# Routing the last batch in two groups of half a batch, unchecked expert ids and earlier writes of q and k, in a fused attention and mixture-of-experts kernel

## The reference

```
x1 = layernorm(x + attention(x))
scores = sigmoid(x1 @ router_weight.T)            # 16 experts, in 4 groups of 4
# the best 2 groups by scores + bias, in them the best 4 experts: tidx
tw = scores[tidx] / sum(scores[tidx]) * 2.5
h_e = silu(x1 @ gate_w[e].T) * (x1 @ up_w[e].T)   # 128 wide, for each expert e
out = layernorm(x1 + sum over the 4 chosen of tw * (h_e @ down_w[e].T)
                   + shared(x1))                   # 2 shared experts, for every token
```

## Time and profile before

| | us |
|---|---|
| median of three runs | 1260.3 |
| lowest and highest | 1251.3 and 1264.51 |
| profiled execution, its own time | 1256.9 |
| its span in the profile | 1254.9 |
| PE busy, share of the span | 1056.3, 84% |
| DVE busy | 863.1, 69% |
| ACT busy | 626.5, 50% |
| POOL busy | 469.5, 37% |

### The profile page before, as it was taken

How to read it: one execution, slowest core, us unless ns; L and a number is a source line. 1 busy time by engine, 2 the same in 40 slices (tenths; PEclk the granted TensorE clock), 3 DMA queues, 4 the chain that set the end, 5 groups by cost and what they waited for, 6 DMA issues and landing times.

```text
span 1254.9 us, 24541 instructions
## 1 busy us (share of the span) xinstructions
PE 1056.3 (84%) x8451; PEld 590.1 (47%) x8451; DVE 863.1 (69%) x1833; ACT 626.5 (50%) x1409; POOL 469.5 (37%) x682
## 2 busy tenths in 40 slices
PE   7696999989777998988997779888898776998895
PEld 4353333344422555544554445454555445654463
DVE  6486787777884666788667676687567556587453
ACT  4323677766444555654555456554455463322332
POOL 7552111152156102223444633214625630286332
PEclk9897999999897999999999899999999898998998
DMA  5753257420123433234366634232636643443320
GB/s 177 214 173 109 69 198 267 125 68 26 49 89 116 62 92 76 58 71 97 98 155 113 169 75 89 61 76 79 150 94 137 181 104 70 136 121 107 90 76 21
DMA packets 181078, 136.07 MB, mean 108 GB/s; under 512 B 105152, under 2 KB 156096, under 8 KB 180960
## 3 DMA queue, kind: packets, MB, share of 16 engines
q1 hardware_dynamic: 170112, 106.17, 33.2%
q0 software_dynamic: 9216, 25.18, 6.4%
q10 hardware_dynamic: 1632, 3.15, 0.9%
HBM read 54.55 MB, written 60.88 MB: 92 GB/s over the span
## 4 chain that ended last, share of the span: by engine, by line
PE 50%; DVE 17%; POOL 12%; issue 11%; ACT 5%; SPq 3%; DMA 2%; DVEq 0%; POOLq 0%; ACTq 0%
PE bank L752 10%; PE bank L575 10%; PE bank L559 8%; PE bank L546 7%; DVE a_mx L1275 5%; POOL a_pool L1076 4%; PE bank L765 3%; PE bank L709 2%; POOL a_QS L1068 2%; POOL rows L1061 2%; ACT a_PT L1137 2%; POOL a_PT L1020 2%; PE bank L659 1%; SPq L838 1%; PE bank L723 1%
## 5 line engine op out<-in xcount | busy, mean ns | idle before, releaser
L1275 DVE TENSOR_REDUCE a_mx<-bank 128x1 f32<-128x512 f32 (+3 forms) x720 | 423.8, 619 | 224.2 <-PE bank L549 144.9
L1137 ACT ACTIVATE a_PT<-bank 128x512 f32<-128x512 f32 (+4 forms) x832 | 374.7, 497 | 224.9 <-PE bank L559 221.3
L559 PE MATMUL bank<-a_QS,a_KS 113*128 113x512 f16 (+4 forms) x832 | 279.8, 344 | 40.3 <-DVE a_mx L1275 32.7
L1020 POOL TENSOR_SCALAR_AFFINE_SELECT a_PT<-a_PT 128x256 f32<-128x256 f32 (+1 forms) x288 | 111.5, 394 | 471.8 <-ACT a_PT L1137 471.1
L546 PE MATMUL bank<-a_KS,a_QS 112*128 112x512 f16 (+4 forms) x832 | 264.6, 340 | 10.4 <-DMA a_KS<-k_dram 5.6
L575 PE MATMUL bank<-a_PT,a_VG 128*17 128x512 f32 (+4 forms) x1664 | 188.3, 527 | 26.6 <-POOL a_PT L1020 26.6
L752 PE MATMUL bank<-e_xt,a_W 128*128 128x128 f16 x1728 | 139.6, 231 | 40.1 <-issue 28.7
L752 PEld LDWEIGHTS bank<-e_xt,a_W 128*128 x1728 | 118.5, 102 | 67.9 <-issue 52.4
L559 PEld LDWEIGHTS bank<-a_QS,a_KS 113*128 113x128 f16 x832 | 82.8, 101 | 121.6 <-DVE a_mx L1275 65.4
L546 PEld LDWEIGHTS bank<-a_KS,a_QS 112*128 112x128 f16 x832 | 81.2, 100 | 103.0 <-ACT a_PT L1137 64.5
L1223 ACT ACTIVATE e_tq<-bank 128x256 f32<-128x256 f32 x96 | 36.8, 383 | 173.1 <-PE bank L752 172.9
(11 more groups left out here) (176 smaller groups left out, 1476.8 us busy)
## 6 DMA issues: line engine op xcount, KB each, us to landing
outs<-e_ys SPq DMA_DIRECT2D x72, 256.0 KB, 2.9
rows<-a_pool SPq DMA_DIRECT2D x48, 256.0 KB, 3.2
a_QS<-c_dram SPq DMA_DIRECT2D x32, 256.0 KB, 3.3
q_dram<-p_qk SPq DMA_DIRECT2D x32, 128.0 KB, 2.1
k_dram<-p_qk SPq DMA_DIRECT2D x32, 128.0 KB, 2.3
v_dram<-p_vs SPq DMA_DIRECT2D x8, 512.0 KB, 3.6
a_QS<-q_dram SPq DMA_DIRECT2D x64, 64.0 KB
a_KS<-k_dram SPq DMA_DIRECT2D x64, 64.0 KB
```

The lines of the kernel that those rows point to most:

```text
L559: pe.matmul(ps[:, 0:(qc + 1) * CH - q0], KS[p][0:MR + 1, kt // NT, h % 2, kt % NT * P:kt % NT * P + P], QS[p][0:MR + 1, qc, h, q0 - qc * C ...
L1020: pool.affine_select(out=a, in_=a, compare_op=ALU.is_ge, fill=0.0, base=q0 - (kt * P - WIN), pattern=[[0, 2], [1, w]], channel_multiplier= ...
L1137: act.activation(PT[(G + i) % 2][:, h, 0:w], bank("ST", G, i, h)[:, 0:w], ACT.Exp)\
L1275: dve.tensor_reduce(mx[:, piece, t // NT, heads[0]:heads[0] + n, t % NT], bank("S", G, u)[:, 0:n * w].rearrange("p (h k) -> p h k", h=n), ...
```

## The change

1. The last batch is routed, in two groups of its own, one for each chunk: 4 tiles, 16 full units of choices and 16 partly filled ones, 32 units, 16 pairs. The five groups are `GROUPS`; the dense jobs (`up`, `down`, `cT`, `dgate`, `load_c` and the rest) are gone. `slot`, `expert` and `wk` get a third buffer.
2. From h = 416 on `fill` takes turns in seven banks, and the pairs from `LATE` on load their rows into 8 tiles that lie in the softmax's buffers PT, which are free once the attention has ended.
3. `load_experts` leaves out the check of the ids against 0 and 15.
4. SP writes chunks 2, 3 and 4 ahead of `stack(0, 0)`.
5. In the first four rounds S takes banks 0 to 2, ST banks 3 to 5, and `fill` bank 7 alone.

```diff
+GROUPS = [(b, 0, BT) for b in range(B - 1)] + [(B - 1, half * NT, NT) for half in range(NH2)]
+UNITS_OF = [TOPK * n + NE for _, _, n in GROUPS]
...
             def load_experts(b, n):
                 on.wait_ge(f["unit_done"], b + 1)
                 _, regs = nc.values_load_multi_w_load_instructions(
-                    expert[b % 2][0:1, n:n + REGS], engines=[mybir.EngineType.PE], min_val=0, max_val=NE - 1)
+                    expert[b % 3][0:1, n:n + REGS], engines=[mybir.EngineType.PE], min_val=0, max_val=NE - 1,
+                    skip_runtime_bounds_check_because="the ids are counts of experts that are held to at most NE - 1")
...
-    RINGS = {"scores": [0, 1, 2, 3, 4], "other": [5, 7], "project": [5, 6, 7], "gates": [0, 1], "ups": [2, 3],
-             "sum0": [4], "sum1": [6]}
+    RINGS = {"s_first": [0, 1, 2], "st_first": [3, 4, 5], "first": [7], "scores": [0, 1, 2, 3, 4], "other": [5, 7], "project": [5, 6, 7], "gates": [0, 1], "ups": [2, 3],
+             "end": [5, 7, 0, 1, 2, 3, 4]}
...
-                ring = "other"
+                ring = "first" if h < 2 * NG * NSL else "other" if h < 2 * ATT else "end"
...
+    def rows_in(i):
+
+        if i < LATE:
+            return xt[i % NXT][:], xt_loaded[i % NXT], i // NXT * 16 + 16, i - NXT
+        j = i - LATE
+        return late_tiles[j % NXL], xt_late[j % NXL], j // NXL * 16 + 16, i - NXL if j >= NXL else -1
...
+            for c in range(2, 5):
+                project(c)
             for p in range(2):
                 sp.wait_ge(qk_written[p], 128)
                 sp.wait_ge(v_written[p], 16)
...
-            for c in range(2, NC - 1):
+            for c in range(5, NC - 1):
                 project(c)
...
+    w = 0
+    for g in range(NGR):
+        at = max(last[g] + 6, w)
+        if g == B - 2:
+            at = max(at, routed[NGR - 1] + 1)
```

More of the change, by code:

```diff
@@ L86, in share, with chunk_of, shared_place @@
     return [((n - TAIL) % NU, n >= TAIL) for n in range(lo, hi)]
[L89 to L99, removed]
+def chunk_of(g, tile):
+    b, j0, _ = GROUPS[g]
+    return b * NH2 + (j0 + tile) // NT
+def shared_place(g, n):
+    return chunk_of(g, n // NSH * 2), n // NSH * 2 % NT
 def plan():
@@ L169, in plan @@
     ready, routed = {}, {}
[L170 to L177, removed]
+    for g, (b, j0, tiles_) in enumerate(GROUPS):
+        late = b == B - 1
+        for c in sorted({chunk_of(g, t) for t in range(tiles_)}):
+            e = span * (b + 1) + ((3 if late else 6) if c % NH2 else -9)
+            sp[e - 1 if not late else tail - 14].append(("load_res", c))
+            pool[e + 4 if not late else tail - 10].append(("add_bo", c))
+            ready[c], at = chain(c, e, 0 if c == NC - 2 else 1)
+        gap = 1 if late else 2
@@ L186, in plan @@
[L186 to L198, removed]
@@ L200, in plan @@
-    wanted, order = [], {}
[L201 to L219, removed]
+                pool[q + 4 + (t * TOPK + k) * 2 // 3].append(("scatter", g, t, k))
@@ new lines, in plan @@
+        routed[g] = q + 4 + tiles_ * TOPK * 2 // 3
+    wanted, order = [], {}
+    for g in range(NGR):
+        for n in range(NPS[g]):
+            c, tile = shared_place(g, n)
+            wanted.append((ready[c] + tile * 5, g, n))
+        lo = routed[g] + 5
+        hi = routed[g + 1] - 7 if g + 2 < NGR and g < B - 2 else tail if g == B - 2 else lo
+        wanted += [(lo + (hi - lo) * n // NPR[g], g, NPS[g] + n) for n in range(NPR[g])]
+    q, last, second, gu_at = -1, {}, [], []
+    for h, g, n in sorted(wanted):
+        order[g, n] = len(order)
+        q = put(("gu", g, n), max([h, q + 1] + [y + 1 for y in second[1 - NHB:2 - NHB]]))
+        gu_at.append(q)
+        act[q].append(("tanh", g, n))
+        dve[q + 1].append(("gate", g, n))
+        act[q + 2].append(("hh", g, n))
+        dve[q + 3].append(("hl", g, n))
+        if n >= NPS[g]:
+            sp[q - (5 if q < tail + 10 else 10)].append(("load_rows", g, n))
+            last[g] = y = put(("y", g, n), q + (5 if q < tail else 7))
@@ L220, in plan @@
             second.append(y)
-            act[y + 1].append(("y_out", b, n))
-            sp[y + 3].append(("store_y", b, n))
+            act[y + 1].append(("y_out", g, n))
+            sp[y + 3].append(("store_y", g, n))
         elif n % NSH:
-            y = put(("ysh", b, n), q + 5)
+            y = put(("ysh", g, n), q + (5 if q < tail else 7))
             second += [y, y]
-            dve[y + 1].append(("add_shared", b, n))
-    for b in range(NSB):
-        at = last[b] + 6
-        for t in range(BT):
+            dve[y + 1].append(("add_shared", g, n))
@@ L541, in scores @@
                         on.wait_ge(stacked[half][p], k * 128 + 128)
-                ps = take("scores", "S", G, u)
+                ps = take("s_first" if round_of[0] < NG else "scores", "S", G, u)
                 for n, h in enumerate(heads):
@@ L557, in scoresT @@
                     on.wait_ge(negmax[qc][p], k * 16 + 16)
-                ps = take("scores", "ST", G, i, h)
+                ps = take("st_first" if G < NG else "scores", "ST", G, i, h)
                 pe.matmul(ps[:, 0:(qc + 1) * CH - q0],
@@ L617, in project @@
                         maxT("project", 0, 0)
-            experts, sums = {}, []
+            experts = {}
             def load_experts(b, n):
@@ L1369, in route @@
                         link(dve.max_index(i8[:, j, :], m8[:, j, :], sc[:, j, :]), j % 2)
-                elif part == 4:
+                else:
                     kk = is_k[:, j0:j0 + n]
```

413 lines of the change are left out of this document (143 added, 270 removed).

## The result

| | before | after |
|---|---|---|
| median of 5 runs each, us | 1260.8 | 1217.6 |
| profiled execution, span | 1254.9 | 1209.3 |
| first a_OTs copied by ACT | 125.1 | 123.3 |
| second copy of round 5 (no id loaded yet) | 384.2 | 382.0 |
| last copy, the end of the attention | 1026.6 | 986.1 |

The ratio is 0.966, with a 95% interval of 0.961 to 0.970: 43 us faster. The forecast was 1228 with a range of 1200 to 1250, so time and sign came true. The parts did not. The profiled execution of after was the shortest of its five (1211.1 us), and its span is 45.6 us shorter than that of before; 40.5 of these are gone before the tail begins, where the sum had 15 + 6. The tail, for which the change was mainly written, gave 5 where the sum had 11.

The account below looks back on a forecast made before the run. TensorE was taken to set the pace nearly everywhere, with DVE not far off. Start -6, rings 0, loads -15 and tail -11 made -32 from the profiled 1256.9, so 1224.9, or 1228 as a median; range 1200 to 1250.

Parts of the forecast that it names:

- The loads, -15: Unchecked ids: 1.31 us less for each of 15 loads in the attention, three quarters paid; -15 us, bounds -20 and -8.
- DVE would be the next limit: Attention's loads: DVE, busy in 45 of 60 us, turns some time won into later waits, so three quarters were taken.
- The start, -6: Chunks 2 to 4 written before the stack: 9 us won, less 2.5 for three S banks; -6 us, bounds -9 and 0.
- The three banks of S: At the start, TensorE reaches the next projection half a microsecond late for DVE, 5 of 12 times; costs 2.5 us.
- The rings, 0: Split of the banks in rounds 0 to 3: no net effect, 0 us, bounds -5 and +5.
- The tail, -11: Routed last batch behind the attention: the tail ends at 1244, 11 us earlier; bounds -21 and about 0.
- TensorE's pace: Tail: a pair's gu takes 2.19 us when pairs follow one another, 91 ns for a product of 128 columns.
- the end chain: From the last y: output, store, 16 gathers, combine, statistics, norm and the rest to the end of the span, 41 us.
- 16 us of lag less the 6 or so: Tail: combines wait for batch 2's gathers; less what seven banks and six hh buffers let TensorE run ahead, 10 us.
- the bound of -21: The tail's gain if the 10 us lag of combines behind gathers falls away.
- Rival (b): Tail runs better than laid out, without the 10 us lag, and loads pay in full: about 1213; chance 0.22.
- (d): Routed tail: TensorE was never its limit, lag eats the 11 us; start and loads alone pay: 1248 to 1262; chance 0.08.

Follow-up runs that it names:

- no_route: Kernel before, last batch still dense, with unchecked ids, early writes and split rings: 1217.5 us, ratio 0.966, second chip.
- after_again: The changed kernel unaltered, run again beside the kernel before on the second chip: 1218.5 us against 1261.8, ratio 0.966.
- end_two: The changed kernel with two banks instead of seven for the expert work behind the attention: 1233.7 us, ratio 0.977, second chip.
- tail_paced_2: The changed kernel with batch 2's gathers planned one per half slot, 4 half slots later, so combines stand further back: 1202.7 us, ratio 0.953, third chip.
- old_rings: The changed kernel with the banks of rounds 0 to 3 taken as before: 1288.4 us, ratio 1.005, first chip.
- plain_tail: The changed kernel with indirect transfers behind the attention replaced by plain ones of the same sizes: 1198.5 us, ratio 0.949, third chip.

## Why the forecast was right, and where its working was wrong

**The loads, -15.** This step failed. It took "8 x 0.164 = 1.31" as the price of the check and then three quarters of it. The price is the spacing, 2.3 us for each load, and on the chips of the result and of no_route nothing was hidden: from the second copy of round 5 to the first of round 15 after needs 570.1 us (382.0 to 952.1) and before 605.5 (384.2 to 989.7), 35.4 less for the 15 loads in it, 2.4 for each. no_route needs 570.3 for it, and from round 5 on the ids are the only part of the change in its attention, so that they alone explain it. That is beyond the term's own bound of -20. On the first chip the ids gave less, 1.5 to 1.6 us for each load; what took the rest there is not shown. The row that told it was at hand: the idle time of 2.70 us in the earlier trace rows, from which 1.31 was taken and 1.39 left, when 0.46 to 0.76 was what stayed. The argument that DVE would be the next limit found no support.

**The start, -6.** Right in mechanism and size for the writes (6 to 7 us on the first chip). The wait for the stack took the place of the one that went, as laid out. The three banks of S cost 4 to 5 at the first copy in place of 2.5. With both, 2.2 us were left at round 5 in the profile of after and 1.5 to 4.9 in the other five of the second and third chip, where the two terms had 6.

**The rings, 0.** In its bounds, as a gain and a loss that cancel. The lead of after over before is 1.8 us at the first copy, 6.0 at the end of round 2 and 3.1 at the end of round 3 and 2.2 at round 5, the same course as in the pairs on the first chip; the rows of 144 to 186 show 0.7 us more work in 42 us.

**The tail, -11.** Two of its numbers held: TensorE's pace (24 products in some 2.1 to 2.2 us at full clock where pairs follow one another, with 2.19 forecast) and the end chain (39.8 for 41, though the items that the prediction lists for it add up to 39.4). One did not: "16 us of lag less the 6 or so" was 10 and the waits for `hl` took 20.7 us (26.7 in all of the tail of after_again). The banks did their part and more, 15 us in end_two. What the term had only in its bounds, and apart from the lag, is that a lag comes with less clock: 0.78 was granted in those 54 us, so that a part of the work ran at 1.2 GHz in place of 2.4. The last `y` came 183.7 us behind the attention's end, where 176 were forecast. With the waits inside that stretch removed, in tail_paced_2, the tail is 210.7 us, 17.6 under before, near the bound of -21 that the prediction gave for it. As built, routing is worth 5 us in one profile and 1 in the other, and since the dense tail with unchecked ids also takes 225, next to nothing of that is the routing's.

So the loads gave 20 us more than forecast, and the tail 6 to 10 less and the start with the rings 1 to 5 less. That these errors have opposite signs, and left only 10 us between 1228 and 1217.6, is luck. Rival (b) had the loads "in full", but at 1.31 us each, 20 in all, and the tail wrongly; (d) had the tail nearly rightly and the loads at 15.

The Trainium skill, "TensorE: Matmul & The Clock Gate", section "Back-to-back issue gap", gives 81 ns for a sustained product of 128 columns. Of after, two pairs that follow one another, one pair behind other work, when the list had run ahead, both at a granted clock of 1.00, and the register operations of all `gu` (ns):

```profile
1135.13 4.29 PE L711 MATMUL bank<-a_PT,a_W 128*128 128x128 f16 x48
1011.35 1.50 PE L711 MATMUL bank<-a_PT,a_W 128*128 128x128 f16 x24
L711 PEldq FUSED_REGOPS  x1664: 46/46/46, 403.2 to 1164.6; - x185
```

That is 89 ns and 63 ns for one product; the page's figure lies between. The 91 of the earlier trace rows did not go with the check: the register operations on the line of `gu`, 16 for each routed pair, are in after as they were in before, and pairs in a row keep nearly their price (the 91 had been measured at a granted clock of 0.81).

## What to carry to other kernels

Cost a group of sequencer instructions from its first start to its last end, in a window that holds only one of them; the sum of their durations can miss half. Before an engine is relieved of work, look for the in-order list in which a waiting step stands ahead of what that engine needs: here eight combines were planned at three gathers for two half slots, which is 0.95 us a gather by the 2.84 us of a pair (an estimate), where a gather takes 1.26. Planning one gather for each half slot, and four half slots later, brought some 15 us, on a chip like that of the result and with the changed kernel measured on another; on the first chip no gain was seen. And when a change has several parts, run it without its largest one.

## What the runs showed of the hardware

**One chip slows TensorE and ACT where POOL issues indirect transfers.** In old_rings, on the first chip, the tail is 263 us where it is 223 and 227 in the changed kernel on the others. Its waits from 1026 on ("remote" is a releaser that the trace doesn't know):

```profile
DVE e_ga L1418 <- ACT e_tq L1147: 43.3, 18, 12.6
ACT e_tq L1147 <- remote: 40.1, 8, 7.7
...
PE bank L711 <- issue: 34.2, 45, 1.9
```

Two stretches of it, the first inside a run of scatters and gathers, the second between two such runs:

```profile
1091.00:1118.00 27.00, 11.52 (x40) 3.95 (x38) 2.45 (x6) 2.55 (x6) 18.04 (x19) 0.58 0.66 174
1121.00:1130.00 9.00, 9.00 (x111) 8.09 (x110) 7.03 (x17) 2.94 (x8) 0.00 (x0) 0.92 0.33 59
```

With 19 indirect transfers TensorE has 40 products in 27 us, without one 111 in 9. Its timeline there, the products being of a shared expert, with no register in them:

```profile
1099.39 0.37 PE L736 MATMUL bank<-a_W,e_hh 128*128 128x256 f16 x1 [1.06 <-issue]
1100.10 0.37 PE L736 MATMUL bank<-a_W,e_hh 128*128 128x256 f16 x1 [0.34 <-issue]
...
1101.49 0.37 PE L736 MATMUL bank<-a_W,e_hl 128*128 128x256 f16 x1 [1.02 <-issue]
```

SP issued nothing from 1089.0 to 1097.17. Its line below holds two stores of 0.36 us, as short as elsewhere, and the 5.3 us between them: each starts within 0.03 us of the end of the copy by ACT that it waits for. So these rows show ACT late, by waits of 4.30 and 4.77 us for a releaser that the trace doesn't know, and no slowness of SP's own. In the whole tail such waits of ACT sum to 72 us, and to 71 to 79 in the other three kernels with a routed last batch on that chip; in after and on the other two chips there are none. POOL kept its pace of 1.26.

```profile
1096.55 0.60 ACT L1162 ACTIVATE e_ys<-bank 128x512 f32<-128x512 f32 x1 [4.30 <-remote]
1102.20 0.60 ACT L1162 ACTIVATE e_ys<-bank 128x512 f32<-128x512 f32 x1 [4.77 <-remote]
1097.17 6.02 SPq L879 DMA_DIRECT2D outs<-e_ys  x2
```

The DMA engines are less busy in those 27 us (0.66) than in after between 1058 and 1112 (0.83), where none of this is seen; TensorE's waits of that kind sum to 67 us in the whole of old_rings, and to 5.7 in after, 5.3 in after_again and 3.0 in no_route. It was seen in each of the four kernels on that chip whose last batch is routed (54 to 106 us, the last with the checks' own), and with 20 to 25 us in the three that route three batches, which have no scatters in the tail. These three also lose time in the attention: from the second copy of round 5 to the first of round 15 they need 597 to 604 us, with unchecked ids, where after and the runs on the other two chips need 570 to 573. In old_rings 62 of the 67 us lie inside runs of indirect transfers or at most 1.5 us from one, and these runs fill a quarter of the span. That it is the issuing of indirect transfers that does it rests on their falling together in time; plain_tail was meant to test it and came to a chip without the effect. The cause, and why one chip has it, stays open.

**Waits and clock go together.** The stretch from 1058 to 1112 was granted 0.78 with six waits of TensorE for `hl` in it (20.7 us) and 0.97 in tail_paced_2 without them. TensorE's level is 1.2 or 2.4 GHz, so 0.78 is 44% of the time at the lower one. The three stretches of after in which the lower level was granted:

```profile
1064.70:1071.53 6.83, 4.36 (x30) 3.66 (x31) 6.10 (x16) 1.45 (x4) 5.30 (x6) 0.50 0.73 178
1085.18:1092.01 6.83, 4.43 (x23) 3.04 (x24) 4.01 (x11) 2.90 (x7) 5.17 (x9) 0.50 0.21 61
1098.84:1109.08 10.24, 4.47 (x36) 3.85 (x37) 4.70 (x11) 2.15 (x5) 1.73 (x2) 0.50 1.12 245
```

Each begins inside a wait of TensorE for `hl` that had begun before it (at 1060.71, 1083.52 and 1098.55), so here the wait came first. TensorE worked 13.3 of these 23.9 us, at half its clock.

**Plain and indirect transfers of POOL differ in issue, not in kind.** The Trainium skill, "DMA: Bandwidth & Descriptors", section "SWDGE vs HWDGE vs iDMA", says that a transfer issued by GpSimd, plain or indirect, is described in software; the page of plain_tail agrees, with the 12288 packets of the software queue that the changed kernel has too. What differs is 0.53 us against 1.26 for one.
